# A four-layer graph network on one core: layer 3 reads stored keys instead of edge records, and the summing stage before it writes them

## The reference

```python
e_h, e_t, e_r = h[src], h[dst], rel[type]
score = sum(e_t * tanh(e_h + e_r), axis=-1)
w = exp(score - max(score))
attn = w / (segment_sum(w, src)[src] + 1e-10)
agg = segment_sum(attn[:, None] * e_t, src)
x = x + leaky_relu((h + agg) @ W.T, 0.2)
```

## Time and profile before

| | |
|---|---|
| median of 3 runs | 11995.28 us |
| profiled execution | 12014.41 us, span 12012.6 |
| PE busy | 8140.2 us, 68% |
| DVE busy | 8287.7 us, 69% |
| POOL busy | 6896.0 us, 57% |
| ACT busy | 4862.3 us, 40% |
| layer 1's sums | 5196 to 5887 us |
| layer 3 | 9140 to 11902 us |

### The profile page before, as it was taken

The page is one execution under the profiler, slowest core; times in us unless marked ns, Lnnn a source line. Parts: engine busy times, 40 slices in busy tenths (PEclk is TensorE's granted clock), DMA queues, the critical chain, the costliest instruction groups (busy, mean ns, idle before and its releaser), DMA issues. The chain is left out here.

```text
span 12012.6 us, 257271 instructions
## 1 busy us (share of the span) xinstructions
PE 8140.2 (68%) x63022; PEld 6349.2 (53%) x63685; DVE 8287.7 (69%) x33874; ACT 4862.3 (40%) x9481; POOL 6896.0 (57%) x7087
## 2 busy tenths in 40 slices
PE   0222222255888888867766777777755999999996
PEld 0222222234566555556545666666653777777775
DVE  7444444426888888878526999999987666666664
ACT  3000000003777777722103555555542444444442
POOL 1777777722777777720004777777753666666662
PEclk9999999998888888889857999999987999999997
DMA  3333333330222222146301222222252333333345
GB/s 116 80 80 80 80 80 80 78 29 24 61 60 59 59 58 58 50 121 175 104 11 34 60 59 60 60 59 60 60 46 64 98 99 98 98 99 98 98 97 59
DMA packets 863125, 886.04 MB, mean 74 GB/s; under 512 B 466669, under 2 KB 636430, under 8 KB 862693
## 3 DMA queue, kind: packets, MB, share of 16 engines
q0 software_dynamic: 254464, 511.95, 18.7%
q1 hardware_dynamic: 608613, 373.57, 12.0%
HBM read 699.65 MB, written 155.84 MB: 71 GB/s over the span
## 5 line engine op out<-in xcount | busy, mean ns | idle before, releaser
L1291 POOL DMA_INDIRECT a_far<-node_table,a_rows x3552 | 3464.3, 975 | 3242.7 <-DMA a_rows<-edge_records 1256.1
L1069 POOL DMA_INDIRECT message_records<-f_msg,f_index x1760 | 1746.3, 992 | 924.2 <-issue 528.1
L897 POOL DMA_INDIRECT sum_far<-split_table,sum_rows x1760 | 1669.2, 948 | 669.4 <-issue 631.9
L982 PE MATMUL banks<-sum_far,sum_hot 128*128 128x128 bf16 x5280 | 635.5, 310 | 1711.8 <-DMA sum_far<-split_table,sum_rows 1604.8
L982 PEld LDWEIGHTS banks<-sum_far,sum_hot 128*128 128x128 bf16 x5280 | 528.2, 143 | 1819.0 <-issue 891.1
L964 ACT ACTIVATE acc<-sum_cur 128x128 f32 x880 | 272.2, 309 | 2752.8 <-DVE sum_cur L926 2415.6
L926 DVE SCALAR_TENSOR_TENSOR sum_cur<-sum_cur,gsame,banks 128x128 f32<-128x128 f32 x880 | 303.0, 344 | 1253.6 <-PE banks L982 1250.5
L1429 PE MATMUL banks<-ident,a_score 128*128 128x128 f32 x7072 | 997.1, 287 | 223.2 <-DVE a_score L1351 197.5
L1449 PE MATMUL banks<-a_far,a_prob 128*128 128x129 f32 x7056 | 1029.6, 291 | 0.0
L1429 PEld LDWEIGHTS banks<-ident,a_score 128*128 128x128 f32 x7072 | 994.5, 202 | 32.3
L1393 ACT ACTIVATE a_hot_t<-banks 128x512 bf16<-128x512 bf16 x888 | 521.4, 587 | 1038.6 <-PE banks L1438 749.9
(11 more groups left out here) (271 smaller groups left out, 19179.5 us busy)
## 6 DMA issues: line engine op xcount, KB each, us to landing
a_rows<-message_records SPq DMA_DIRECT2D x446, 264.0 KB
sum_rows<-message_records SPq DMA_DIRECT2D x441, 264.0 KB
acc<-a_cur SPq DMA_DIRECT2D x880, 65.0 KB
a_far<-node_table,a_rows POOLq DMA_INDIRECT x3552
sum_far<-split_table,sum_rows POOLq DMA_INDIRECT x1760
message_records<-f_msg,f_index POOLq DMA_INDIRECT x1760
f_attr<-edge_attributes SPq DMA_DIRECT2D x447, 40.0 KB
edge_attributes<-in_edge_attr SPq DMA_DIRECT2D x8, 1953.1 KB, 33.7
```

The costliest lines, as they stand in the source:

```text
L897: pool.indirect_dma_start(far[:, u, q, :], None, k.table3[:, :], bass.IndirectOffsetOnAxis(ap=rows[:, u, q, C_SRC:C_SRC + 1].bitcast(I32), ...
L982: last = nc.tensor.matmul(k.psum[a % 2][:, 0:D], hot[:, u, q, :], rhs, start=q == 0 and part == 0, stop=q == KG - 1 and part == (2 if o == ...
L1069: pool.indirect_dma_start(k.mrec[:, :], bass.IndirectOffsetOnAxis(ap=index[:, u, q:q + 1], axis=0), msg[:, u, q, :], None, bounds_check=ED ...
L1291: pool.indirect_dma_start(far[:, u, q, 0:D], None, k.table[:, :], bass.IndirectOffsetOnAxis(ap=rows[:, u, q, other:other + 1].bitcast(I32) ...
```

## The change

Five things. Names of tiles and stages are those of the diff.

- Layer 1's sums (`segment_sums(k, 1)`) write two new tensors in memory as they go: for each group the source row and the type of its 512 edges in one line of bf16 (`source_keys`), and for each partition 16 floats with the four targets, the mask for edges outside the window, the rows and the types (`source_columns`). For this GpSimd gets three small instructions for each group (`note`), TensorE one turn of eight columns, ScalarE one copy (`take_keys`), SP two stores (`store`); the vector engine waits for the slot's stores before it writes `rel`. 16 groups of zeroes are written ahead of the loop.
- This stage loads three groups ahead (`LOAD` 3) instead of one.
- Layer 3 is a new function, `relation`, in place of `attention(k, 1)`. It loads the keys, broadcast to all 128 partitions, and the columns. The transposed one-hots are made by comparing the broadcast keys with the partition's number, 512 columns at a time: no turn and no copy. The relation rows are split as two products instead of three (`rel2`: high and middle part in one of 128 rows, low part in one of 64).
- One running maximum for all partitions: each partition takes the maximum of its four scores, one fp32 product spreads these 128 numbers, and a maximum over 128 columns follows. The exponentials are taken on the 128x4 scores; the vector engine writes the weighted one-hots in the layout that the sums need (`weigh`), so the weights are not turned.
- Eight slots for most tiles, four for keys and one-hots, leads up to 7, and another order of stages on each engine.

```diff
 def segment_sums(k, o):
-    LOAD, HOT, SUM, ADD = 1, 1, 0, 0
+    LOAD, HOT, SUM, ADD = (3 if o else 1), 1, 0, 0
 # SP
+                    if o:
+                        sp.wait_ge(noted, now(g, a + 1))
                     e0 = first_edge(sp, k, o, g + a)
...
+                def store(g, a):
+                    u, n = a % U, g + a
+                    sp.wait_ge(keys_ready, now(g, 2 + a + 1))
+                    sp.dma_start(k.scols[bass.ds(n * P, P), :], scol[:, u, :]).then_inc(k.keys_out[u], 16)
+                    sp.dma_start(k.skeys[bass.ds(n, 1), :].rearrange("a (r e) -> (a r) e", e=P), skey[:, u, :]).then_inc(k.keys_out[u], 16)
+                    for n in range(NG, NS):
+                        sp.dma_start(k.scols[n * P:(n + 1) * P, :], none[:, :]).then_inc(k.stored, 16)
+                        sp.dma_start(k.skeys[n, :].rearrange("(p q) -> p q", p=P), none[:, 0:KG].bitcast(BF16)).then_inc(k.stored, 16)
+                    sp.wait_ge(k.stored, s_stored + 32 * (NS - NG))
+                skewed(sp, (LOAD, load), *(((SUM, store),) if o else ()), counts=now, turn=2 * U)
 # GpSimd
+                    def note(g, a):
+                        u = a % U
+                        pool.wait_ge(k.rows_in[u], now(g, s_row[u] + 16 * (a // U + 1), 16 // U))
+                        pool.wait_ge(k.keys_out[u], now(g, 32 * (a // U + 1), 32 // U))
+                        pool.sem_inc(k.begun, 1)
+                        nc.gpsimd.tensor_copy(scol[:, u, COL_DST:COL_DST + KG].bitcast(I32), rows[:, u, :, M_DST].bitcast(I32))
+                        nc.gpsimd.tensor_copy(scol[:, u, COL_KIND:COL_KIND + KG], rows[:, u, :, M_TYPE].bitcast(I32)).then_inc(noted, 1)
+                        pool.wait_ge(rel_ready, now(g, s_rel + a + 1))
+                        pool.sem_inc(k.begun, 1)
+                        nc.gpsimd.tensor_scalar(scol[:, u, COL_HIDE:COL_HIDE + KG], scol[:, u, COL_REL:COL_REL + KG], float(P), -BIG,
+                                                ALU.is_ge, ALU.mult).then_inc(hidden, 1)
+                    skewed(pool, (SUM, note), counts=now, turn=2 * U)
 # DVE, one_hot
+                    if o:
+                        dve.wait_ge(k.keys_out[u], now(g, 32 * (a // U + 1), 32 // U))
 # ACT
+                def take_keys(g, a):
+                    u = a % U
+                    act.wait_ge(keys_turned, now(g, a + 1))
+                    act.wait_ge(k.keys_out[u], now(g, 32 * (a // U + 1), 32 // U))
+                    nc.scalar.activation(skey[:, u, :], k.psum[2 + a % 2][0:2 * KG, 0:P], ACT.Copy).then_inc(keys_ready, 1)
+                skewed(act, (ADD, keep), *(((SUM, take_keys),) if o else ()), counts=now, turn=2 * U)
 # PE, after total's sums
+                    if o:
+                        pe.wait_ge(noted, now(g, U + a + 1))
+                        pe.wait_ge(hidden, now(g, 1 + a + 1))
+                        pe.wait_ge(keys_ready, now(g, a + 1))
+                        nc.tensor.transpose(k.psum[2 + a % 2][0:2 * KG, 0:P], scol[:, u, COL_REL:COL_REL + 2 * KG], k.ident[:, :])\
+                            .then_inc(keys_turned, 1)
...
-        attention(k, 1)
+        relation(k)
...
+def relation(k):
+    LOAD, GATHER, HOT, NEAR, SCORE, MAX, WEIGH, ADD = 7, 6, 5, 4, 3, 2, 1, 0
+    S, H = 2 * U, 4
...
+                def load(g, a):
+                    wait(sp, now, keys_taken, g, a, H)
+                    wait(sp, now, prob_ready, g, a, S)
+                    n = g + a
+                    sp.dma_start(keys[:, a % H, :], k.skeys[bass.ds(n, 1), :].broadcast_to([P, 2 * GE])).then_inc(loads_in[a % S], 16)
+                    sp.dma_start(cols[:, a % S, :], k.scols[bass.ds(n * P, P), :]).then_inc(loads_in[a % S], 16)
+                skewed(sp, (LOAD, load), (ADD, keep), counts=now, turn=S)
...
+                def gather(g, a):
+                    u = a % S
+                    pool.wait_ge(loads_in[u], slot_count(now, g, a, 32, S))
+                    wait(pool, now, summed, g, a, S)
+                    for q in range(KG):
+                        pool.indirect_dma_start(
+                            far[:, u, q, 0:D], None, k.table[:, :],
+                            bass.IndirectOffsetOnAxis(ap=cols[:, u, COL_DST + q:COL_DST + q + 1].bitcast(I32), axis=0))\
+                            .then_inc(gathered[u], 16)
...
+                def one_hots(g, a):
+                    nc.vector.tensor_scalar(hot_t[:, h, :], keys[:, h, 0:GE], k.part_id[:, 0:1], None, ALU.is_equal)
+                    nc.vector.tensor_scalar(kind_t[:, h, :], keys[:, h, GE:], k.part_id[:, 1:2], None, ALU.is_equal)\
+                        .then_inc(onehotT_ready, 1)
...
+                def score_edges(g, a):
+                    for q in range(KG):
+                        last = nc.vector.scalar_tensor_tensor(
+                            work[:, q, :], near_ps[b][:, q * D:(q + 1) * D], 1.0, far[:, u, q, 0:D], ALU.mult, ALU.mult,
+                            accum_out=raw[:, q:q + 1])
...
+                    nc.vector.tensor_tensor(score[:, u, :], raw[:, :], cols[:, u, COL_HIDE:COL_HIDE + KG], ALU.add).then_inc(masked, 1)
+                    nc.vector.tensor_reduce(peak[:, u:u + 1], score[:, u, :], AX, ALU.max).then_inc(scores, 1)
...
+                    nc.vector.tensor_reduce(gmax[:, :], peak_ps[a % 2][:, 0:P], AX, ALU.max).then_inc(group_max, 1)
...
+                def weigh(g, a):
+                    for q in range(KG):
+                        last = nc.vector.tensor_scalar(share[:, b, q, :], k.iota_b[:, :], cols[:, u, COL_REL + q:COL_REL + q + 1],
+                                                       prob[:, u, q:q + 1], ALU.is_equal, ALU.mult)
...
+                skewed(dve, (HOT, one_hots), (ADD, add), (WEIGH, weigh), (SCORE, score_edges), (MAX, running_max), counts=now, turn=S)
...
+                skewed(act, (MAX, exps), (NEAR, terms), counts=now, turn=S)
...
+                skewed(pe, (MAX, spreads), (NEAR, near), (WEIGH, sums), counts=now, turn=S)
```

More of the change, by code:

```diff
@@ L147, in link @@
             eng.wait_ge(chain, linked[0])
-        n_loads = len(weights) + len(rows) + len(wide) + 3
+        n_loads = len(weights) + len(rows) + len(wide) + 4
         with nc.Block() as block:
@@ L161, in _ @@
                 sp.dma_start(bf1[:, :], b_f1.rearrange("(n a) -> n a", a=1)).then_inc(loaded, 16)
-                sp.dma_start(rel_f[:, :], rel).then_inc(loaded, 16)
+                for half in range(2):
+                    sp.dma_start(rel_f[half * NTYPE:(half + 1) * NTYPE, :], rel).then_inc(loaded, 16)
                 sp.wait_ge(loaded, 16 * n_loads)
@@ L223, in program @@
             "edge_term", "near_ready", "in1", "in2", "in3", "edge_dot", "scores", "spread", "group_max", "kinds_ready", "kept",
+            "keys_taken", "masked", "noted", "hidden", "keys_turned", "keys_ready",
             "exp_in", "weighed", "shrink", "prob_turned", "prob_ready")}
         k.rows_in = [sem(f"rows_in{u}") for u in range(U)]
+        k.keys_out = [sem(f"keys_out{u}") for u in range(U)]
+        k.loads_in, k.gathered = ([sem(f"{n}{u}") for u in range(2 * U)] for n in ("loads_in", "gathered"))
         k.pool_done = [sem(f"pool_done{u}") for u in range(U)]
@@ L860, in segment_sums @@
         cur = k.sb(own, f"sum_cur{o}", [P, U, D])
+        noted, hidden, keys_turned, keys_ready = (st[x] for x in ("noted", "hidden", "keys_turned", "keys_ready"))
+        if o:
+            scol, skey = k.sb(own, "sum_cols", [P, U, COLS]), k.sb(own, "sum_keys", [2 * KG, U, P], BF16)
+            none = k.sb(own, "sum_none", [P, COLS])
+            assert not any(k.since(x) for x in (noted, hidden, keys_turned, keys_ready, *k.keys_out))
         if o == 0:
@@ L877, in load @@
                         .then_inc(k.rows_in[a % U], 16)
-                skewed(sp, (LOAD, load), counts=now, turn=2 * U)
+                def store(g, a):
[4 more added lines that the diff above has]
+                if o:
+                    for u in range(U):
+                        sp.sem_inc(k.keys_out[u], 32)
+                    sp.wait_ge(hidden, 1)
+                    for n in range(NG, NS):
[3 more added lines that the diff above has]
+                skewed(sp, (LOAD, load), *(((SUM, store),) if o else ()), counts=now, turn=2 * U)
+                if o:
+                    for u in range(U):
+                        sp.wait_ge(k.keys_out[u], 32 * (1 + NG // U))
                 if o == 0:
@@ L917, in one_hot @@
                     for q in range(KG):
-                        last = nc.vector.tensor_scalar(hot[:, u, q, :], k.iota_b[:, :], rel[:, u, q:q + 1], None, ALU.is_equal)
+                        last = nc.vector.tensor_scalar(hot[:, u, q, :], k.iota_b[:, :], near[:, q:q + 1], None, ALU.is_equal)
                     last.then_inc(onehot_ready, 1)
@@ L988, in segment_sums @@
     k.since.passed(NG + 2, added)
+    if o:
+        k.since.passed(NG + U, noted)
+        k.since.passed(NG + 1, hidden)
+        k.since.passed(NG, keys_turned)
```

(3 more changed lines are left out.)

183 lines of the change are left out of this document (171 added, 12 removed).

## The result

| | before | after |
|---|---|---|
| median, us | 11996.35 (4 runs, 11993.59 to 12001.31) | 12095.17 (4 runs, 12086.25 to 12099.84) |
| ratio, 95% interval | | 1.0081 [1.0064, 1.0098] |
| profiled execution, us | 12014.41 (span 12012.6) | 12095.22 (span 12093.5) |
| second summing stage, first vector instruction to the next step's first, us | 691.8 | 1205.8 |
| the same per group in mid-stage, us | 1.544 | 2.68 |

The forecast was 11789, its range ended at 11960, and slower had 0.10. The kernel lies 306 us above the forecast. The difference between the two profiled executions, +81 us, is +514 in the summing stage, -427 in layer 3 (counted from the first clearing instruction of each) and -6 elsewhere.

What follows compares the result with a forecast made beforehand. The tensor engine was taken to bound layer 3, the vector engine layer 2 and, with 1.43 us of back to back work, the second summing stage. 12014.4 - 512 + 304 + 2 = 11808, less 19: 11789 us; range 11590 to 11960.

Steps and rivals of the forecast that it cites:

- I take 2.20 us a group, between the two; SP then binds and the vector engine idles.: Second summing stage: SP's queue, with two added stores, sets 2.20 us a group; stage 994 us, a loss of 304.
- Both readings that bounded my value, 2.25 and 2.08: SP's time a group, summing stage: 1.31 + 0.94 = 2.25 with two stores, or 2.08 for three transfers with a register load.
- the two waits that are new here: SP's queue in the second summing stage: two added waits, which the 2.08 us reading for three transfers does not contain.
- Below 2.20, so it is hidden by SP: Second summing stage: the store's own chain takes 5.1 us for three groups, 1.70 a group, below SP's 2.20.
- Rival (4): Second summing stage: SP and chain add up, 7.4 us for three groups, 2.47 a group, total 11908; chance 0.13.
- The loads three groups ahead ... move nothing past SP's own work: Second summing stage: longer load distance takes away waits for a transfer; the sum gives it nothing.
- Zero stores: Ahead of the second summing stage's loop: 32 stores of zeroes at 0.43 with 1.5 to land, 15 us.
- GpSimd's small instructions: Second summing stage: three instructions of four columns at 0.2 us each, 0.6 a group, beside the rest.
- I take 5.01 us a group: Layer 3: GpSimd's four gathers, 948 ns each plus 0.305 us gap, set 5.01 us a group.
- rival (5): Layer 3: the vector engine binds at 6.0 us a group, gain only 88 us, total 12213; chance 0.11.
- 446 x 5.01: Layer 3: the loop gathers 440 + 6 groups at 5.01 us each, 2234 us of the stage's 2245.
- Rival (3): Layer 3: gathers slowed to 1009 ns as in layer 2, 5.26 us a group, total 11899; chance 0.12.

## Why the prediction was wrong

The miss of 306 us has four parts: +210 in the summing stage, +85 in layer 3, -8 elsewhere, and +19 because the kernel before was profiled 19 us above its median, which I took off, and the kernel after at its median.

**The step that failed: "I take 2.20 us a group, between the two; SP then binds and the vector engine idles."** That SP binds was right, as was what the trace would show then, an SP with hardly any wait. Its size was wrong: 2.68 a group, 0.48 x 440 = 211 us. The single load's share (1.31 from the earlier trace rows) held: 1.30 to 1.33 where loads stand alone. What was mis-sized is the two stores: 0.51 and 0.43 from the earlier trace rows, 1.3 to 1.4 measured. In the timeline only 0.57 and 0.52 stand between the entries; the rest hides in the way back to the next load, 1.49 and up to 1.8. Both readings that bounded my value, 2.25 and 2.08, took the price of a further transfer from the start of the message stage, whose transfers follow each other without a wait between them (2872.32 to 2872.75). They don't cover a store with waits of its own in a full loop. Which part of such an entry costs the difference, its waits or something else, no run separates. A range from those two rows left the true value outside; I named "the two waits that are new here" and gave them no price.

**"Below 2.20, so it is hidden by SP" failed too, without a price of its own.** The chain counts 8.05 us for three groups, not 5.1. My sum began at the store and ended at the next slot's use; it left out that the next load stands behind that store in SP's queue, and then needs 1.5 to be issued and 2.97 to land. Rival (4) had this kind of mechanism, SP and chain in one loop, with 2.47. It is a second wall at the same place: shortening the loop (by the copies' order, by eight slots) brought 38 and 1 us; with the stores batched as well it was 426.

**"The loads three groups ahead ... move nothing past SP's own work"** held at three. Two ahead would be 587 us slower, so the distance is needed to stay at SP's pace. Three loads ahead in the kernel before alone were not tried; its vector engine waits 24.3 us for loads in the 400 us from 5400, 0.09 a group, so there was little to gain.

**Zero stores.** 18 us from the first to the first load (15 forecast). **GpSimd's small instructions** lie beside the rest, 0.18 to 0.30 us each (0.2 forecast).

**Layer 3** went as forecast in its middle: "I take 5.01 us a group", measured 5.05, gathers at 958 ns with 0.30 between. Cost groups of 9800 to 11500 us, answering and the earlier trace rows:

```profile
L1634 POOL DMA_INDIRECT r_far<-node_table,r_cols x1347 | 1290.3, 958 | 410.5 <-issue 391.3 <-DMA r_cols<-source_columns 19.2
...
L1695 DVE TENSOR_SCALAR r_share<-iota_b,r_cols,r_prob 128x128 f32<-128x128 bf16 x1348 | 377.7, 348 | 0.0
...
L1666 DVE SCALAR_TENSOR_TENSOR r_work<-banks,r_far 128x128 f32<-128x128 f32 x1344 | 310.4, 287 | 209.2 <-DMA r_far<-node_table,r_cols 207.8
...
L1654 DVE TENSOR_SCALAR r_hot_t<-r_keys,part_id 128x512 bf16<-128x512 bf16 x337 | 121.5, 360 | 18.7 <-issue 17.8
```

The compare of 512 columns takes the 0.36 us worked out from 0.25 ns a column. The weighted fp32 one-hots take 1.11 for four in a row (0.87 forecast, upper end 1.40). The vector engine is 75% busy, forecast "near 85%", and waits mostly for a gathered transfer, as it should; rival (5) fell. The tensor engine is 86% busy, 4.36 us a group, forecast "near 65%" and 3.25. A part is the clock of 0.81: with three gathers and a clock of 0.97 the same products take 3.81. The other 0.56 was priced too low: the spread, for one, is two products of 0.49 together, forecast at 0.29. It never bound: with three gathers it has the same work a group, and the turn is shorter.

The gain was 427 instead of 512. 54 of the missing 85 are the padding tail: my 446 x 5.01 gave every group one price. A look at the last 100 us of each stage before would have shown it: the DMA share is 0.81 in 11780 to 11900 of the kernel before. The rest is 17 for a gather pace of 5.048 instead of 5.01 (446 groups, from the run with spread padding) and 14 for draining: 18.5 us from the end of the last gather's turn to the output step in that run, forecast at 5.

**Rival (3)**, slowed gathers, had 1009 ns from layer 2; measured is 958, 12 above. The Trainium skill, GPSIMD Engine Reference, section Specifications, speaks of contention with VectorE's two-port modes and two-input instructions on the shared interface. The traces agree with the direction between before and after, 946 beside a vector engine 69% busy and 958 beside one 75% busy, but with three gathers it is 954 beside one 85% busy. No run shows how much of the 12 ns is contention.

## What to carry to other kernels

A DMA queue's engine is an engine with a busy time, though no row of the profile counts it: price an added transfer by the start-to-start time in a loop that has the same waits and register loads, not by the gap between two issues in a row, and look at what is queued behind a new wait before calling a chain short. A small store issued once for several groups costs its queue a fraction: here, with the eight slots that it needs and the keys copied first, it turned a loss of 0.8% into a gain of 2.8% over the kernel before. Multiply a group's price only by the groups that are alike, and look at the last slices of each stage for those that aren't.

## What the runs showed of the hardware

- **Gathers of one row.** Where all 128 indices of a gather name the same row, the DMA engines are 0.89 busy at 80 GB/s in layer 3 and a group of four gathers takes 7.0 us on average; with 64 different rows, each twice, it is 5.0 us at a share of 0.40 and 117 GB/s. In the first case one gather takes 21 us of the 16 engines' time instead of 3.9, and loads behind it land late: the DMA engines, not GpSimd, then set the pace.
- **A store in a full queue.** A load alone takes SP 1.31 us, the first small store adds 0.63 and the second 0.7 to 0.8, while the entries of the two stores stand 0.52 apart. The 32 stores of zeroes, back to back without waits, took 0.4 to 0.5 us each (5193.30 to 5209.10, 15.8 us with one gap of 1.6).
- **The tensor engine's granted clock.** It was 1.00 in the summing stage before (turn 1.544), 0.71 after (turn 2.68), 0.58 with two loads ahead (turn 4.0), 0.94 with only the key store batched (turn 2.14), 0.98 with both batched (turn 1.69). In these runs the longer it waited for its data in a turn of the same work, the lower was its clock, and one group's sums take 2.08 us at 1.2 GHz where those of the group three turns later take 1.16. The busy time a group rises by this, 1.87 us after (278 us for 149 groups) against 1.16 before (300 for 259, without the added turn of the keys), and looks like load where there is none. One stage doesn't fit: in the first summing stage, 300 to 2400 us of the kernel after, the clock is 1.00 with the engine 29% busy. What sets it stays open.
